# Mixture-of-experts tiles on one core: the down projection one tile later, and each transpose in front of a bf16 product

## The chip, the cores and the metric

The kernel runs on one core of a Trainium2 chip. A core has a matrix engine (TensorE, PE in the profile, with its weight loads as PEld), a vector engine (VectorE, DVE), a scalar engine (ScalarE, ACT), GpSimd (POOL), and SyncE (SP), which here only issues DMAs. Each engine works through its own list of instructions in order and waits on semaphores that the others raise. The metric is the device time of one execution in microseconds (us).

## The reference, cut to what matters

Eight sequences of 256 tokens of width 256 first pass a layer norm and a retention-like attention over a context. Then comes the part that this case is about, a layer of eight experts of which each token uses two:

```python
scores = softmax(xf @ Wg.T)                        # 2048 tokens, 8 experts
expert_weights, expert_indices = top_k(scores, 2)  # normalised to sum 1
h1 = xf @ W1[e].T + (xf @ A1[e].T) @ B1[e].T + b1[e]   # 256 -> 512
h3 = xf @ W3[e].T + (xf @ A3[e].T) @ B3[e].T + b3[e]   # 256 -> 512
g  = silu(h1) * h3
y_e = g @ W2[e].T + (g @ A2[e].T) @ B2[e].T + b2[e]    # 512 -> 256
y  = sum over the two experts of weight * y_e
x  = x + tanh(g_ffn) * y
```

## The kernel before

**The first stage** (to about 112 us) runs the attention for the eight sequences. Beside it the low-rank factors are folded into the expert weights: DVE adds a product of the factors to a staged weight unit, ACT rounds the sum to WH (`weight_hi`, L752), and POOL takes the rest as a bf16 part WL (`weight_lo`, L992). The six units of the last expert (number 7) are folded inside the first three expert tiles.

**The second stage** sorts the 4096 token-expert pairs by expert and works on 39 tiles (`NT_SLOTS`) of 128 rows, tile i with one expert. For one tile:

- POOL gathers 128 normalised rows of xn2 from memory into one of four buffers `xg` by an indirect DMA (`gather`, L1034 and L1056).
- PE transposes them, two f32 transposes of 128x128 into bank 0 (L630). ACT copies the result as a rounded `xh` (L877) and as bf16 `xb` (L878), and DVE takes the rest `xl` (L1493). There are two sets of these.
- PE forms h1 in bank 1 and h3 in bank 2 (`up`, L640). Each is six products of 512 columns: two with xh, two with xl, both against WH, and two with bf16 xb against WL.
- DVE adds the biases (L1503), ACT applies silu (L945), DVE multiplies into `g` (L1509).
- PE transposes g, four f32 transposes into bank 3 (L648). ACT makes `gh` (L883) and bf16 `gb` (L887), DVE the rest `gl` (L1497). There is one set of these.
- PE forms y in bank 4 (`down`, L657): twelve products of 256 columns, four each with gh, gl and gb.
- ACT has put the scaled output bias in `ys` (`scaled_bias`, L929), DVE adds y times the gate (`result`, L1515), and POOL adds the 128 rows to the output in memory with an indirect DMA (`scatter`, L1067 for its column of row numbers, L1079 for the DMA).

**What orders the work.** Everything is written out by hand; each engine has a function `tile(i, ...)` that is called for i = 0 to 38. On PE a step is: h1 of tile i, the transposes of g of tile i-1, the transposes of x of tile i+1, h3 of tile i, down of tile i-1. On POOL a step is the gather for tile i+3, in the first three steps a pair of `weight_lo` of the last expert, and the scatter of tile i-1. Two rules tie the scatters to the rest. A scatter waits until the scatter before it has landed (`pool.wait_ge(s_scat[1 - p], ...)`), since both add to rows in memory. And `ys` has two buffers, so that `scaled_bias` of a tile waits until the scatter of two tiles before has landed:

```python
if i >= 2:
    act.wait_ge(s_scat[p], 16 * half(i, p))
nc.scalar.activation(ys[p][:], b2, ACT.Copy, scale=gs[q]).then_inc(s_b2g, 1)
```

SP loads one row set of biases per tile for the first 16 tiles (`load_biases`, a broadcast to 128 partitions), and then the biases of all eight experts one after the other; from tile 5 on each such load also waits for the scatter of five tiles before. In step 4 ACT loads two tables of functions, once for exp and once back for silu.

Of the kernel before, what the change touches and what calls it, by code (L numbers as in the profile page):

```python
# [34 lines left out]
P = 128  # L35
B, S, D = 8, 256, 256
E, HID, R, K = 8, 512, 16, 2
TOK = B * S
NJ = TOK // P
CH = D // P  # L40
HC = HID // P
TPB = S // P
NT_SLOTS = TOK * K // P + E - 1
XBUF = 4
# [36 lines left out]
def flamingo(nc, x, ctxT, wqkv, tables, mask, gates_in, w_all, lora, biases, wgT, ident_in, consts, out):  # L81
# [9 lines left out]
    with whole:  # L91
# [255 lines left out]
        def _(sp):  # L347
# [63 lines left out]
            def load_biases(i):  # L411
# [21 lines left out]
                else:  # L433
                    sp.wait_ge(s_h3b, i - BRING + 1)
                    sp.wait_ge(s_b2g, i - BRING + 1)
                if i == 4:
                    sp.wait_ge(s_scat[0], 16)
                if i > BRING:
# [32 lines left out]
        def _(pe):  # L471
# [150 lines left out]

            def x_transposes(i, q):
                pe.wait_ge(s_xg[q], 16 * ((i - q) // XBUF + 1))
                if i > 0:
                    pe.wait_ge(s_xh, i)
                    pe.wait_ge(s_xb, i)
                    pe.wait_ge(s_xl, i)
                for c in range(CH):
                    last = nc.tensor.transpose(pX[:, c * P:(c + 1) * P], xg[q][:, c * P:(c + 1) * P], ident[:])  # L630
                last.then_inc(s_xT, 1)

            def up(dst, i, p, e, kind, sig):

                pos_wait(pe, s_h1b if kind == 0 else s_h3b, i)
                for part, (lhs, W, ready) in enumerate(((xh, WH, s_xh), (xl, WH, s_xl), (xb, WL, s_xb))):
                    if kind == 0:
                        pe.wait_ge(ready, i + 1)
                    for c in range(CH):
                        last = nc.tensor.matmul(dst[:, :], lhs[p][:, c * P:(c + 1) * P],  # L640
                                                W[:, bass.ds(e * (UNITS * UC) + (2 * kind + c) * UC, HID)],
                                                start=(part == 0 and c == 0), stop=(part == 2 and c == CH - 1))
                last.then_inc(sig, 1)

            def g_transposes(i):
                pe.wait_ge(s_g, i + 1)
                for c in range(HC):
                    last = nc.tensor.transpose(pG[:, c * P:(c + 1) * P], g[:, c * P:(c + 1) * P], ident[:])  # L648
                last.then_inc(s_gT, 1)

            def down(i, e):

                pos_wait(pe, s_ys, i)
                for part, (lhs, W, ready) in enumerate(((gh, WH, s_gh), (gl, WH, s_gl), (gb, WL, s_gb))):
                    pe.wait_ge(ready, i + 1)
                    for c in range(HC):
                        last = nc.tensor.matmul(pY[:, 0:D], lhs[:, c * P:(c + 1) * P],  # L657
                                                W[:, bass.ds(e * (UNITS * UC) + 4 * UC + c * D, D)],
                                                start=(part == 0 and c == 0), stop=(part == 2 and c == HC - 1))
                last.then_inc(s_y, 1)  # L660
# [12 lines left out]
            def tile(i, q, first, more):  # L673
                p = q % 2
                up(pH1, i, p, expert(q), 0, s_h1)
                if not first:
                    g_transposes(i - 1)
                if more:
                    x_transposes(i + 1, (q + 1) % XBUF)
                if first:  # L680
                    pe.wait_ge(s_wl, (E - 2) * UNITS + 4)
                up(pH3, i, p, expert(q), 1, s_h3)
                if more:
                    read_expert(i + 1, (q + 1) % XBUF)
                if not first:
                    if i == 1:
                        pe.wait_ge(s_wl, (E - 1) * UNITS)
                    down(i - 1, expert((q - 1) % XBUF))
                if i == 0:
# [23 lines left out]
            read_expert(0, 0)  # L713
            x_transposes(0, 0)
            keep_clock(4, WL, pS)
            pe.wait_ge(s_wl, (E - 2) * UNITS + 2)
            pe.wait_ge(s_top, 2 * (B - 1))
            tile_steps(pe, tile)
            g_transposes(NT_SLOTS - 1)
            down(NT_SLOTS - 1, expert((NT_SLOTS - 1) % XBUF))  # L720


        @block.scalar
        def _(act):
# [206 lines left out]
            def tile(i, q, first, more):  # L931
                p = q % 2
                v, at = places
                if not first:
                    g_high(i - 1)
                if more:
                    x_parts(i + 1, 1 - p)
                first_gate(i, q, v)
                if not first:
                    g_short(i - 1)  # L940
                if i == 2:
                    act.wait_ge(s_xn2Tp, B)
                    copy_xn2T(pO)
                act.wait_ge(s_h1b, i + 1)
                nc.scalar.activation(h1[:], h1[:], ACT.Silu).then_inc(s_silu, 1)  # L945
                both_gates(i, q, v)
                if not first:
# [41 lines left out]
        def _(pool):  # L989
# [102 lines left out]
            for i in range(NT_SLOTS):  # L1092
                if i + XBUF - 1 < NT_SLOTS:
                    gather(i + XBUF - 1)
                if i < 3:
                    weight_lo(E - 1, 1, 2 * i)
                    weight_lo(E - 1, 1, 2 * i + 1)
                if i >= 1:
                    scatter(i - 1)
            scatter(NT_SLOTS - 1)  # L1100
# [3 lines left out]
        def _(dve):  # L1104
# [412 lines left out]
            def tile(i, q, first, more):  # L1517
# [8 lines left out]
                biased(h1, pH1, i, x, 0, s_h1, s_h1b)  # L1526
                if not first:
                    g_rest(i - 1)
                if more:
                    x_rest(i + 1, 1 - p)  # L1530
                beside_h3(i)
                product(i, x)
                if not first:
                    result(i - 1, (q - 1) % XBUF)

            dve.wait_ge(s_x2, B)
            variance(st2, mv2, s_mv2, sums(x2, st2))
            x_rest(0, 0)
            tile_steps(dve, tile)
            g_rest(NT_SLOTS - 1)  # L1540
            result(NT_SLOTS - 1, (NT_SLOTS - 1) % XBUF)
# [71 lines left out]
```

## Time and profile before

| what | value |
|---|---|
| device time, median of three runs | 330.6 us (329.95 to 330.95) |
| span of the profiled execution, first to last instruction | 325.4 us |
| PE busy | 297.9 us, 92% of the span |
| DVE busy | 248.2 us, 76% |
| ACT busy | 206.0 us, 63% |
| POOL busy | 210.8 us, 65% |
| scatters | 39, each 1.66 us on POOL; POOL stood idle before them for 58.4 us in all |

The device time holds some 5.2 us that lie outside the span. Busy times are shares of the whole span and mix the two stages. A line of the profile gives engine, line of the kernel, operation and what is written from what. Ends of matmuls are modelled, so that the distance between two starts is the safer reading; where a row groups several matmuls, its start is that of the first.

### The profile page before, as it was taken

The page shows a single profiled execution, that of the slowest core. Times are in us where ns is not written, and L with a number is a line of the kernel's source. Part 1 is how long each engine was busy: PE and PEld are TensorE (multiplying, and loading weights), DVE is VectorE, ACT ScalarE, POOL GpSimd, SP SyncE. Part 2 cuts the span into 40 slices and gives each one's busy share as a digit, 9 for nine tenths or more (in the row PEclk, how much of TensorE's full clock was granted, in tenths as well). Part 3 has the DMA queues.
Part 4 walks back from the last instruction along what each step waited for, and adds up shares of the span by engine and source line. Part 5 has one row for each costly group of instructions (what it writes and reads, how often), then busy time and mean ns, then how long its engine had stood idle before and what let it go on. Part 6 is the DMA issues. An engine that isn't in the chain of part 4 may idle for free. (4 is left out here: it accounts for less than half of the span.)

```text
span 325.4 us, 7435 instructions
## 1 busy us (share of the span) xinstructions
PE 297.9 (92%) x1755; PEld 230.0 (71%) x1755; DVE 248.2 (76%) x607; ACT 206.0 (63%) x486; POOL 210.8 (65%) x246
## 2 busy tenths in 40 slices
PE   7589989999997798999999999999999999999960
PEld 3468778788886656776777777777777777777740
DVE  2679879889999998697988976767776776777750
ACT  5635755766878577787675565665675665675550
POOL 2457878888893098866756656766577776666241
PEclk9799999999999699999999999999999999999996
DMA  7968997999972169567747675766533223333100
GB/s 265 391 158 240 280 297 253 294 279 278 278 244 85 17 225 296 138 201 200 205 139 206 175 187 186 175 187 197 148 56 55 52 51 66 53 45 61 20 0 0
DMA packets 30424, 54.35 MB, mean 167 GB/s; under 512 B 7232, under 2 KB 15808, under 8 KB 30112
## 3 DMA queue, kind: packets, MB, share of 16 engines
q1 hardware_dynamic: 14672, 36.10, 34.1%
q0 software_dynamic: 7488, 9.36, 16.7%
q10 hardware_dynamic: 8224, 8.42, 8.6%
q8 instruction: 17, 0.28, 0.4%
q14 instruction: 23, 0.19, 0.2%
HBM read 41.92 MB, written 10.65 MB: 162 GB/s over the span
## 5 line engine op out<-in xcount | busy, mean ns | idle before, releaser
L1079 POOL DMA_INDIRECT out<-ys,cols x39 | 64.7, 1660 | 58.4 <-DMA out<-ys,cols 33.0
L883 ACT ACTIVATE gh<-bank 128x512 fp32r<-128x512 f32 x39 | 23.4, 599 | 61.0 <-PE bank L648 61.0
L640 PE MATMUL bank<-WH,xh 128*128 x156 | 55.7, 438 | 0.1
L1056 POOL DMA_INDIRECT xg<-xn_rows,colg x39 | 40.0, 1026 | 20.5 <-POOL colg L1034 10.3
L992 POOL TENSOR_TENSOR WL<-stage,WH 128x512 bf16<-128x512 f32 x38 | 47.9, 1278 | 7.3 <-ACT WH L752 7.1
L640 PE MATMUL bank<-WH,xl 128*128 x156 | 49.0, 395 | 0.0
L640 PE MATMUL bank<-WL,xb 128*128 x156 | 47.2, 385 | 0.0
L752 ACT ACTIVATE WH<-stage 128x512 fp32r<-128x512 f32 x38 | 22.9, 628 | 17.7 <-DVE stage L1110 14.5
L640 PEld LDWEIGHTS bank<-WH,xl 128*128 128x128 f32 x156 | 29.2, 188 | 6.8 <-DVE xl L1493 0.4
L1497 DVE TENSOR_TENSOR gl<-bank,gh 128x512 fp32r<-128x512 f32 x39 | 26.9, 689 | 8.8 <-ACT gh L883 8.7
L657 PE MATMUL bank<-WH,gh 128*128 x156 | 32.0, 327 | 1.5 <-ACT gh L883 1.5
L1509 DVE TENSOR_TENSOR g<-g,h 128x512 f32<-128x512 f32 x39 | 27.1, 694 | 5.0 <-ACT h L945 1.1
L1503 DVE TENSOR_TENSOR h<-bank,BA 128x512 f32<-128x512 f32 x23 | 15.9, 691 | 19.3 <-PE bank L640 18.1
L657 PEld LDWEIGHTS bank<-WH,gh 128*128 128x128 f32 x156 | 24.0, 190 | 7.7 <-issue 2.7
L1110 DVE TENSOR_TENSOR stage<-bank,stage 128x512 f32<-128x512 f32 x38 | 24.6, 676 | 0.9 <-DMA stage<-w_all_in 0.9
L657 PE MATMUL bank<-WH,gl 128*128 x156 | 24.9, 281 | 0.4 <-DVE gl L1497 0.4
L640 PEld LDWEIGHTS bank<-WH,xh 128*128 128x128 f32 x156 | 24.0, 190 | 1.7 <-issue 0.7
L648 PEld LDWEIGHTS bank<-ident,g 128*128 128x128 f32 x156 | 19.3, 140 | 8.1 <-DVE g L1509 1.1
L887 ACT ACTIVATE gb<-gh 128x512 bf16<-128x512 f32 x39 | 24.9, 638 | 0.0
L945 ACT ACTIVATE h<-h 128x512 f32<-128x512 f32 x39 | 24.9, 638 | 0.0
L640 PEld LDWEIGHTS bank<-WL,xb 128*128 128x128 bf16 x156 | 9.0, 98 | 21.3 <-issue 21.3
L657 PE MATMUL bank<-WL,gb 128*128 x156 | 23.8, 275 | 0.0
(229 smaller groups left out, 702.2 us busy)
## 6 DMA issues: line engine op xcount, KB each, us to landing
BB<-biases_in SPq DMA_DIRECT2D x16, 640.0 KB, 4.1
stage<-w_all_in SPq DMA_DIRECT2D x38, 256.0 KB, 5.1
BA<-biases_in SPq DMA_DIRECT2D x8, 640.0 KB, 3.9
WL<-w_all_in SPq DMA_DIRECT2D x10, 256.0 KB, 4.7
LS<-WH SPq DMA_DIRECT2D x45, 48.0 KB
xn_rows<-xn ACTq DMA_DIRECT2D x8, 256.0 KB, 4.1
out<-x ACTq DMA_DIRECT2D x7, 256.0 KB, 3.1
cx<-ctxT_in ACTq DMA_DIRECT2D x6, 256.0 KB, 6.5
```

Source lines behind the costliest of these rows:

```text
L640: last = nc.tensor.matmul(dst[:, :], lhs[p][:, c * P:(c + 1) * P], W[:, bass.ds(e * (UNITS * UC) + (2 * kind + c) * UC, HID)], start=(part ...
L657: last = nc.tensor.matmul(pY[:, 0:D], lhs[:, c * P:(c + 1) * P], W[:, bass.ds(e * (UNITS * UC) + 4 * UC + c * D, D)], start=(part == 0 and ...
L752: nc.scalar.activation(w_dst(WH, s, m), stage[stage_of(s * UNITS + m)][:, :], ACT.Copy).then_inc(s_wh, 1)
L883: nc.scalar.activation(gh[:], pG[:, :], ACT.Copy).then_inc(s_gh, 1)
L887: nc.scalar.activation(gb[:], gh[:].bitcast(F32), ACT.Copy).then_inc(s_gb, 1)
L945: nc.scalar.activation(h1[:], h1[:], ACT.Silu).then_inc(s_silu, 1)
L992: nc.gpsimd.tensor_tensor(w_dst(WL, s, m), stage[stage_of(s * UNITS + m)][:, :], w_dst(WH, s, m).bitcast(F32), ALU.subtract).then_inc(s_wl, 1)
L1056: nc.gpsimd.indirect_dma_start(out=xg[q][:], out_offset=None, in_=xn2_d[0:JA * P, :] if i < NA else xn2_d, in_offset=bass.IndirectOffsetOn ...
L1079: nc.gpsimd.indirect_dma_start(out=out_rows, out_offset=bass.IndirectOffsetOnAxis(ap=cols[:, i:i + 1], axis=0), in_=ys[p][:], in_offset=No ...
L1110: nc.vector.tensor_tensor(stage[b][:, :], pW[m % 2][:, :], stage[b][:, :], ALU.add).then_inc(s_add, 1)
L1497: nc.vector.tensor_tensor(gl[:], pG[:, :], gh[:].bitcast(F32), ALU.subtract).then_inc(s_gl, 1)
L1509: nc.vector.tensor_tensor(g[:], g[:], h1[:], ALU.mult).then_inc(s_g, 1)
```

## The change

On PE the down projection of a tile moves one step later and to another place: step i holds h1 of tile i, down of tile i-2, h3 of tile i. The two transposes of x of tile i+1 are no longer a block; each stands in front of one of the two bf16 products of h1. The four transposes of g of tile i-1 stand in front of the four bf16 products of the down projection of tile i-2. After the last step down of tile 37, the transposes of g of tile 38 and its down remain.

On ACT the making of gh and gb of tile i-1 moves from the start of the step and from behind the first gate to a place behind the silu of tile i. On DVE the rest gl of tile i-1 moves behind the result, which is now that of tile i-2, and the product h3 times silu comes last. On POOL the scatter in step i is that of tile i-2. SP drops one wait: the bias load of tile 4 no longer waits for the scatter of tile 0.

```diff
@@ SP, load_biases
-                if i == 4:
-                    sp.wait_ge(s_scat[0], 16)
                 if i > BRING:
                     sp.wait_ge(s_scat[(i - BRING - 1) % 2], 16 * ((i - BRING - 1) // 2 + 1))
@@ PE
+            def x_transpose(i, c):
+                q = i % XBUF
+                if c == 0:
+                    pe.wait_ge(s_xg[q], 16 * ((i - q) // XBUF + 1))
...
+            def g_transpose(i, c):
+                if c == 0:
+                    pe.wait_ge(s_g, i + 1)
...
+            def up(dst, i, p, e, kind, sig, x_next=None):
...
                     for c in range(CH):
+                        if part == 2 and x_next is not None:
+                            x_transpose(x_next, c)
...
-            def down(i, e):
+            def down(i, e, g_next=None):
...
                     for c in range(HC):
+                        if part == 2 and g_next is not None:
+                            g_transpose(g_next, c)
...
             def tile(i, q, first, more):
                 p = q % 2
-                up(pH1, i, p, expert(q), 0, s_h1)
-                if not first:
-                    g_transposes(i - 1)
-                if more:
-                    x_transposes(i + 1, (q + 1) % XBUF)
+                up(pH1, i, p, expert(q), 0, s_h1, i + 1 if more else None)
+                if i == 1:
+                    for c in range(HC):
+                        g_transpose(0, c)
+                if i == 2:
+                    pe.wait_ge(s_wl, (E - 1) * UNITS)
+                if i >= 2:
+                    down(i - 2, expert((q - 2) % XBUF), i - 1)
...
                 up(pH3, i, p, expert(q), 1, s_h3)
...
-                    down(i - 1, expert((q - 1) % XBUF))
...
             tile_steps(pe, tile)
-            g_transposes(NT_SLOTS - 1)
+            down(NT_SLOTS - 2, expert((NT_SLOTS - 2) % XBUF))
+            for c in range(HC):
+                g_transpose(NT_SLOTS - 1, c)
             down(NT_SLOTS - 1, expert((NT_SLOTS - 1) % XBUF))
@@ ACT, tile
-                if not first:
-                    g_high(i - 1)
                 if more:
                     x_parts(i + 1, 1 - p)
                 first_gate(i, q, v)
-                if not first:
-                    g_short(i - 1)
...
                 nc.scalar.activation(h1[:], h1[:], ACT.Silu).then_inc(s_silu, 1)
+                if not first:
+                    g_high(i - 1)
+                    g_short(i - 1)
                 both_gates(i, q, v)
@@ POOL, the loop over tiles
-                if i >= 1:
-                    scatter(i - 1)
+                if i >= 2:
+                    scatter(i - 2)
+            scatter(NT_SLOTS - 2)
             scatter(NT_SLOTS - 1)
@@ DVE, tile
                 biased(h1, pH1, i, x, 0, s_h1, s_h1b)
-                if not first:
-                    g_rest(i - 1)
                 if more:
                     x_rest(i + 1, 1 - p)
                 beside_h3(i)
+                if i >= 2:
+                    result(i - 2, (q - 2) % XBUF)
+                if not first:
+                    g_rest(i - 1)
                 product(i, x)
-                if not first:
-                    result(i - 1, (q - 1) % XBUF)
```

On PE, a late step before, from h1 through the transposes to the start of h3 (bank 1 is h1, bank 2 h3, bank 3 the transposed g, bank 0 the transposed x; ISA sets an address register):

```order
L640 MATMUL bank1<-WH,xl1 128x512 x2
L640 ISA
L640 MATMUL bank1<-WL,xb1 128x512
L640 ISA
L640 MATMUL bank1<-WL,xb1 128x512
L648 MATMUL bank3<-ident,g 128x128 x4
L630 MATMUL bank0<-ident,xg2 128x128 x2
L640 ISA
L640 MATMUL bank2<-WH,xh1 128x512
```

The same place now, from the xl products of h1 to the first product of the down projection (bank 4):

```order
L649 MATMUL bank1<-WH,xl1 128x512 x2
L629 MATMUL bank0<-ident,xg2 128x128
L649 ISA
L649 MATMUL bank1<-WL,xb1 128x512
L629 MATMUL bank0<-ident,xg2 128x128
L649 ISA
L649 MATMUL bank1<-WL,xb1 128x512
L662 ISA
L662 MATMUL bank4<-WH,gh 128x256
```

The two transposes of x have moved from behind h1 into its last third, one in front of each bf16 product, and what follows h1 is now the down projection.

On POOL, the second and third step of the tile loop before, from the second pair of `weight_lo` to the second scatter (xg are gathered rows, colg and cols the row numbers of a gather and of a scatter):

```order
L992 TENSOR_TENSOR WL<-stage,WH 128x512 x2
L1030 TENSOR_LOAD vid
L1030 ISA x2
L1067 ISA
L1067 COPY cols<-sidxA 128x1
L1079 DMA out<-ys,cols 2048x256
L1030 TENSOR_LOAD vid
L1030 ISA x2
L1034 ISA
L1034 COPY colg<-gidxA 128x1
L1056 DMA xg<-xn_rows,colg 128x258
L992 TENSOR_TENSOR WL<-stage,WH 128x512 x2
```

The same place now, from the second pair of `weight_lo` to the first scatter:

```order
L998 TENSOR_TENSOR WL<-stage,WH 128x512 x2
L1036 TENSOR_LOAD vid
L1036 ISA x2
L1040 ISA
L1040 COPY colg<-gidxA 128x1
L1062 DMA xg<-xn_rows,colg 128x258
L998 TENSOR_TENSOR WL<-stage,WH 128x512 x2
L1036 TENSOR_LOAD vid
L1036 ISA x2
L1073 ISA
L1073 COPY cols<-sidxA 128x1
L1085 DMA out<-ys,cols 2048x256
```

The first scatter has moved behind the next gather and behind the third pair of `weight_lo`, to the place that the second scatter had before.

## Rows read from the trace of the kernel before

**Rows 1.** The page, its first line.
```profile
span 325.4 us, 7435 instructions
```

**Rows 2.** Chain of waits, one late step: start us, us, what.
```profile
236.50 0.44 PE bank L648 x4
...
237.16 1.38 PE bank L640 x6
238.54 1.39 PE bank L657 x12
...
241.31 0.44 PE bank L648 x4
```

**Rows 3.** Timeline of PE, before tile 0: start, duration, instruction, [idle <- releaser].
```profile
117.06 0.38 PE L630 MATMUL bank<-ident,xg 128*128 128x128 f32 x2
117.28 1.03 PE L475 MATMUL bank<-WL 128*128 128x512 bf16 x4
```

**Rows 4.** Timeline of PE, three stops in the tile stage.
```profile
125.34 0.44 PE L630 MATMUL bank<-ident,xg 128*128 128x128 f32 x2 [1.44 <-DMA xg<-xn_rows,colg]
...
149.06 0.78 PE L657 MATMUL bank<-WH,gh 128*128 x4 [0.62 <-ACT gh L883]
...
184.90 0.50 PE L657 MATMUL bank<-WH,gl 128*128 x2 [0.41 <-DVE gl L1497]
```

**Rows 5.** Timeline of POOL, the first three scatters and the last pair of weight_lo.
```profile
132.56 1.63 POOL L1079 DMA_INDIRECT out<-ys,cols  x1 [0.95 <-POOL cols L1067]
...
135.86 2.52 POOL L992 TENSOR_TENSOR WL<-stage,WH 128x512 bf16<-128x512 f32 x2
...
139.32 1.60 POOL L1079 DMA_INDIRECT out<-ys,cols  x1 [0.81 <-issue]
...
144.70 1.90 POOL L1079 DMA_INDIRECT out<-ys,cols  x1 [2.07 <-ACT gsel L901]
```

**Rows 6.** Line L1079, issue to landing: all 39 scatters.
```profile
DMA to landing us min/median/max: 2.7/4.1/5.8
```

**Rows 7.** Line L1079, issue to landing: the 16 scatters from 149.3 to 226 us.
```profile
DMA to landing us min/median/max: 3.7/4.7/5.8
```

**Rows 8.** Timeline of POOL, the fourth and the nineteenth scatter.
```profile
149.36 1.60 POOL L1079 DMA_INDIRECT out<-ys,cols  x1 [1.07 <-DMA out<-ys,cols]
...
225.45 1.74 POOL L1079 DMA_INDIRECT out<-ys,cols  x1 [1.16 <-DMA out<-ys,cols]
```

**Rows 9.** Timeline of ACT, end of step 2, then step 4 and start of step 5.
```profile
134.78 1.16 ACT L752 ACTIVATE WH<-stage 128x512 fp32r<-128x512 f32 x2
...
144.54 0.51 ACT L929 ACTIVATE ys<-BB,gsel 128x256 f32<-128x256 f32 x1
...
148.22 0.58 ACT L883 ACTIVATE gh<-bank 128x512 fp32r<-128x512 f32 x1
```

**Rows 10.** Timeline of PE: h3 of tile 6, then transposes of g of tiles 6 and 20.
```profile
152.93 0.71 PE L640 MATMUL bank<-WH,xh 128*128 x2
...
157.17 0.60 PE L648 MATMUL bank<-ident,g 128*128 128x128 f32 x4
...
226.69 0.49 PE L648 MATMUL bank<-ident,g 128*128 128x128 f32 x3
```

**Rows 11.** Groups by line, 207 to 300 us: busy us, mean ns, idle before.
```profile
L1509 DVE TENSOR_TENSOR g<-g,h 128x512 f32<-128x512 f32 x19 | 13.2, 692 | 2.3 <-ACT h L945 0.5
...
L1515 DVE SCALAR_TENSOR_TENSOR ys<-bank,gsel,ys 128x256 f32<-128x256 f32 x19 | 9.2, 484 | 3.1 <-ACT ys L929 2.9
L1493 DVE TENSOR_TENSOR xl<-bank,xh 128x256 fp32r<-128x256 f32 x19 | 8.0, 423 | 0.0
...
L877 ACT ACTIVATE xh<-bank 128x256 fp32r<-128x256 f32 x19 | 7.2, 378 | 0.0
```

**Rows 12.** PE by stretches: us, busy (instructions), granted clock, DMA share, GB/s.
```profile
8.90:12.30 3.40, 0.17 (x2) 1.00 1.04 384
12.30:15.70 3.40, 3.40 (x9) 0.50 1.05 402
```

**Rows 13.** Timeline of POOL, the last scatter but one.
```profile
313.66 1.57 POOL L1079 DMA_INDIRECT out<-ys,cols  x1 [2.79 <-DVE ys L1515]
```

More of the change, by code:

```diff
@@ L621, in _ @@
             pX, pH1, pH3, pG, pY = bank[0], bank[1], bank[2], bank[3], bank[4]
[L623 to L633, printed above, removed]
+            def x_transpose(i, c):
+                q = i % XBUF
+                if c == 0:
+                    pe.wait_ge(s_xg[q], 16 * ((i - q) // XBUF + 1))
+                    if i > 0:
+                        pe.wait_ge(s_xh, i)
+                        pe.wait_ge(s_xb, i)
+                        pe.wait_ge(s_xl, i)
+                turned = nc.tensor.transpose(pX[:, c * P:(c + 1) * P], xg[q][:, c * P:(c + 1) * P], ident[:])
+                if c == CH - 1:
+                    turned.then_inc(s_xT, 1)
+            def g_transpose(i, c):
+                if c == 0:
+                    pe.wait_ge(s_g, i + 1)
+                turned = nc.tensor.transpose(pG[:, c * P:(c + 1) * P], g[:, c * P:(c + 1) * P], ident[:])
+                if c == HC - 1:
+                    turned.then_inc(s_gT, 1)
+            def up(dst, i, p, e, kind, sig, x_next=None):
                 pos_wait(pe, s_h1b if kind == 0 else s_h3b, i)
@@ L643, in up @@
                 last.then_inc(sig, 1)
[L645 to L649, printed above, removed]
-            def down(i, e):
+            def down(i, e, g_next=None):
                 pos_wait(pe, s_ys, i)
@@ L684, in tile @@
                     read_expert(i + 1, (q + 1) % XBUF)
-                if not first:
-                    if i == 1:
-                        pe.wait_ge(s_wl, (E - 1) * UNITS)
-                    down(i - 1, expert((q - 1) % XBUF))
                 if i == 0:
@@ L713, in _ @@
             read_expert(0, 0)
-            x_transposes(0, 0)
+            for c in range(CH):
+                x_transpose(0, c)
             keep_clock(4, WL, pS)
@@ L1531, in tile @@
                 beside_h3(i)
+                if i >= 2:
+                    result(i - 2, (q - 2) % XBUF)
+                if not first:
+                    g_rest(i - 1)
                 product(i, x)
-                if not first:
-                    result(i - 1, (q - 1) % XBUF)
             dve.wait_ge(s_x2, B)
@@ L1539, in _ @@
             tile_steps(dve, tile)
+            result(NT_SLOTS - 2, (NT_SLOTS - 2) % XBUF)
             g_rest(NT_SLOTS - 1)
```

## The prediction, made blind

> **What bounds the kernel now.** I read the page first, then the chain of waits, the timeline of PE for its stops, the timeline of POOL and the landing times of the scatters, and last the timeline of ACT around the one long stop. The chain of waits of a late step [rows 2] shows PE alone: six transposes from 236.50 to 237.16 (0.66 us), six products of h3 (1.38), twelve products of down (1.39), six of h1 (the 1.38 up to 241.31). The step is 4.81 us and nothing in it waits. So PE bounds the late tiles, and only a shorter row of PE instructions makes them faster.
>
> Earlier tiles have a second limit beside it. A scatter may start only when the one before has landed. From the fourth scatter (149.36) to the nineteenth (225.45) nearly every one waits for exactly that [rows 8], fifteen intervals in 76.09 us, 5.07 us each; landing takes 4.7 us there [rows 7]. That chain is slower than a PE step. It stays hidden only as long as the work can run ahead of it, and `ys` has two buffers, so the lead is limited. PE's stops in the tile stage are few: 1.44 us for gathered rows, 0.62 for gh, 0.41 for gl [rows 4].
>
> **The change part by part.**
>
> *Transposes in front of bf16 products.* PE does the same 6 transposes and 24 products per tile. What could be gained is the time that a transpose or a weight load stands exposed. In a block, six transposes take 0.66 us, 0.11 each [rows 2]. The trace has one place where two transposes stand between bf16 products: 117.06 to 117.28, 0.22 for two, the second followed at once by a bf16 product [rows 3]. So a transpose costs 0.11 there too, and moving it frees nothing. What is left is small and of unknown sign: products of one size stand a little apart by what precedes them (twelve of down in 1.39 are 0.116 each, where a transpose takes 0.11 [rows 2]), so that six pairs may be worth 0.03 us per tile either way. I take a gain of 0.015, since the two bf16 groups now follow a transpose instead of a product of another kind.
>
> The Trainium skill (TensorE: Matmul & The Clock Gate, section LDWEIGHTS (loading the stationary operand)) gives a weight load as the number of columns over 1.2 GHz, 107 ns for 128, and in section Back-to-back issue gap about 56 ns for an isolated product of 128 columns; bf16 weights it counts among those that load faster (Weight-path perf modes). By that a block of transposes is held by its loads, each would cost 56 ns between products, and the step would fall by six times 0.05, some 0.3 us (an estimate from that page). The trace does not agree: with a bf16 product behind it instead of another f32 load, the transpose takes 0.11 all the same [rows 3]. What the mechanism would give is the second rival.
>
> *Down two tiles behind.* What it buys is slack. gh, gl and gb of a tile are now needed one h3 and one h1 later, so stops like the 0.62 and the 0.41 [rows 4] should go by themselves. Against that stands the first stop. The transposes of x of tile 2 wait for gathered rows until 125.34 [rows 4]. Before, all of h1 of tile 1 and the transposes of g of tile 0 ran ahead of that stop; now two bf16 products (0.44) and the transposes of g (0.44 [rows 2]) stand behind it: +0.9 us at the start, which is inside the total below.
>
> *The scatters on POOL.* This is the part that decides. The first scatter stood behind the second pair of `weight_lo` and issued at 132.56. Now it stands behind the third pair. That pair ran at 135.86, and the second scatter followed at 139.32 [rows 5]. The pair waits for ACT's last weight units, at 134.78 before [rows 9]; in the new order ACT comes to them at much the same time, since its step 2 hangs on h1 of tile 2 as before. So the first scatter now issues at about 139.0 instead of 132.56: the whole chain of scatters starts one scatter late, about 6.5 us, while the result of a tile comes only some 3.4 us later than before (h1, six transposes and down, 1.38 + 0.66 + 1.39 [rows 2]).
>
> What waits for it: the scaled bias of tile 3 needs the scatter of tile 1 landed. Before, that scatter issued at 139.32 and ACT wrote ys at 144.54 without a stall worth the name [rows 5, 9]. Now: 139.0 plus 4.1 to land [rows 6], 0.4 until the next issue (5.07 less 4.7 [rows 7, 8]; it is the second scatter that counts), plus 4.7, 148.2. Behind that wait on ACT stand the two table loads of step 4: from the ys to the next large instruction it took 148.22 - 144.54 = 3.68 us [rows 9]. And behind these now stands xh of tile 6, which before stood behind gh. So xh starts at 151.9 and is ready at 152.3 (0.38 [rows 11]). PE would want it for h1 of tile 6 at about 149.8 (h3 of tile 6 was at 152.93 [rows 10]; 0.9 later for the start, 0.6 earlier without the stop at 149.06, and 3.43 back over h1, transposes and down), so it stops for 2.5 us. From 152.3 on: DVE has xl after xb at 153.0 (0.42 [rows 11]), h1 ends at 154.2. DVE still has ys (0.48), then gl once gh is there at 153.9, and the two steps of g (0.69 each [rows 11]), to 156.1; PE wants g at 155.1, a second stop of 1.0. Four transposes of g with four bf16 products take 0.9, and h3 of tile 6 starts at 157.0. At that point both kernels have done the same work (down up to tile 4, h1 up to 6); before, it was 152.93 [rows 10]. So +4.1 us; with both landings as short as 3.7 it is +2.7, with one of 5.8 it is +5.2.
>
> *Tiles 6 to 20.* The kernel before takes 157.17 to 226.69 for fourteen steps, 4.97 each, stops and some routing products included [rows 10]. If the chain of scatters holds each step to 5.07, that is +1.4; if it never binds again, the 0.41 stop goes and the transposes give their 0.03 fourteen times, -0.8. I take 0: PE has just lost 4 us to the chain, so it starts with little lead, but the lead that it has then is what the chain needs.
>
> *Tiles 20 to 38, and the end.* The scatters no longer bind there; 18 steps at 0.015 give -0.3. At the end, the scatter of tile 36 now issues when h3 of tile 38 ends instead of one down earlier, and the scatter of tile 37 (before at 313.66, waiting for its own ys [rows 13]) has to wait for its landing; between 0 and +1.2, I take +0.3.
>
> *SP.* The dropped wait lets one bias load go early, which would otherwise sit behind the later first scatter: 0. The bias load of tile 5 still waits for that first scatter, lands about 147.5 and is needed at 146; the DVE idle time between h1 and the result covers it, and if not, it falls into the stop that ACT makes anyway.
>
> Sum: 4.1 + 0 - 0.3 + 0.3 = +4.1. The profiled execution has a span of 325.4 us [rows 1], and with the 5.2 outside it that is the median, 330.6; I forecast 334.7.
>
> **Rivals.**
>
> *1. ACT's slack swallows the late scatter (no change).* For it: x is now transposed early in h1, so xh has nearly three us of lead, and every later use of gh and gl has more than two. If two landings and the gap come to less than 6.6 us, so that the scatter of tile 1 has landed by 145.6, ys is no later than its own place and PE does not stop. That needs 3.1 each; the shortest of all is 2.7, but only at the very end where nothing else moves, and in the bias loads' stretch the least is 3.7 [rows 6, 7]. Then: stops -1.0 [rows 4], transposes -0.6, start +0.9, end +0.3: 330.2.
>
> *2. The transposes are hidden (faster).* Six products of 512 columns take 1.38, 0.23 each [rows 2], so 128 columns by themselves would take a quarter, 0.06; if the other 0.05 of a transpose is a weight load that a long product in front of it can cover, a step falls by 0.3 us wherever PE bounds. If the chain of scatters still costs its 4.1, the gain counts only in the last 18 steps, -5.4: 329.3. Without that cost it would be 38 steps, some -11: 319. It decides from a transpose at 0.09 instead of 0.11 on. Rows 3 speak against it, with a single instance.
>
> *3. The clock falls in the long stop.* Early in the program a stretch with PE busy for 0.17 of 3.4 us was followed by one at a granted clock of 0.50, that is 1.2 GHz, for 3.4 us [rows 12]. Two stops of 3.5 us in all in step 6 come near to it; at half the clock for 3.4 us or twice that, PE falls back by 1.7 to 3.4: 336.4 to 338.1. Against it: before the stop and between the two PE is at work with full products.
>
> *4. The chain keeps binding.* Gathers on POOL stand behind scatters, bias loads wait for scatters of five tiles before; with the chain late by one scatter these become stops of their own in tiles 6 to 20, +1.4 to +4: 336 to 338.6.
>
> **How the numbers follow.** The forecast (332 to 336) has a chance of 0.55, rival 1 (329.6 to 331.6) 0.14, rival 2 (below 329.6) 0.13, rival 3 0.09, rival 4 0.09. Of rival 1 a part falls on either side of 0.3% (1.0 us), which is about what a measurement of this kernel can tell from no change. So faster by over 0.3%: 0.15, within: 0.13, slower: 0.72. The likeliest case alone ranges from 332.0 to 336.0; the range for 8 in 10 goes down to 329.6, into rivals 1 and 2, and up to 338.0, through most of 3 and 4.
>
> **What would show it.** Right: the first scatter issues near 139 instead of 132.6; ACT waits for a scatter before the ys of tile 3 until about 148; PE stands idle for more than 2 us before h1 of tile 6, released by ACT's xh; the transposes of g of tile 6 come some 4 us late in absolute time; late steps of 4.78 to 4.81 us, the transposes still 0.11 behind the product that follows. Wrong: late steps of 4.5 to 4.7 us (rival 2); no stop of PE over 1 us behind step 2, with ACT's wait before that ys under 1 us (rival 1); a granted clock of 0.50 in the tile stage (rival 3). I would be wrong altogether if the third pair of `weight_lo` ran well before 135, since then the chain of scatters would start early enough.

## The result, and the profile after

The changed kernel takes 333.7 us (median of 18 runs, 331.1 to 337.9), the kernel before 330.5 on the same chip (18 runs, 328.0 to 333.1): a ratio of 1.009, with an interval of 1.006 to 1.012, so 2.1 to 3.9 us slower. The forecast was 334.7. Executions of any kernel here that come out over 1.5% above its fastest are left out of the ratios; where few remain, the interval is wide. Single profiles scatter by microseconds, so profiles show below which wait is where, and ratios what it costs.

The page, first line, answering [rows 1]:

```profile
span 331.5 us, 7472 instructions
```

The spans differ by 6.1 us, twice what the times do. 1.7 of it lies ahead of the change (the first transposes of x start at 118.76, before at 117.06 [rows 3]). And in all runs that list both numbers, 1.75 to 3.0 us of the time lie outside the span, not the 5.2 that were taken: the profile of before probably caught a short execution.

Timeline of POOL in the changed kernel, from the third pair of `weight_lo` to the third scatter (start, duration, instruction, [idle before <- what ended it]), answering [rows 5]:

```profile
135.87 2.92 POOL L998 TENSOR_TENSOR WL<-stage,WH 128x512 bf16<-128x512 f32 x2 [1.12 <-ACT WH L759]
...
139.87 1.62 POOL L1085 DMA_INDIRECT out<-ys,cols  x1 [0.95 <-DVE ys L1522]
...
144.04 1.60 POOL L1085 DMA_INDIRECT out<-ys,cols  x1 [0.81 <-DMA out<-ys,cols]
...
148.94 2.06 POOL L1085 DMA_INDIRECT out<-ys,cols  x1 [1.61 <-DMA out<-ys,cols]
```

The first scatter issues at 139.87, where 139.0 was said and 132.56 stood before. Timeline of ACT, steps 3 and 4, answering [rows 9]:

```profile
143.85 0.51 ACT L936 ACTIVATE ys<-BB,gsel 128x256 f32<-128x256 f32 x1 [3.54 <-DMA out<-ys,cols]
...
148.78 0.51 ACT L936 ACTIVATE ys<-BB,gsel 128x256 f32<-128x256 f32 x1 [0.44 <-DMA out<-ys,cols]
149.30 1.28 ACT L971 ACT_TABLE_LOAD   x1
...
151.06 1.28 ACT L974 ACT_TABLE_LOAD   x1
...
152.46 0.37 ACT L884 ACTIVATE xh<-bank 128x256 fp32r<-128x256 f32 x1
```

ACT stands 3.54 us in front of the ys of tile 2, until the first scatter has landed (139.87 and 3.9 to land, 143.8), and 0.44 in front of that of tile 3. The two table loads follow, and only behind them xh of tile 6. Over the whole program ACT's ys now waits nearly five times as long as before (3.8 us in 6 waits there). Waits of the changed kernel: engine, line, what for, us in all, times, longest:

```profile
ACT ys L936 <- DMA out<-ys,cols: 17.7, 16, 3.5
...
PE bank L636 <- DVE g L1516: 4.2, 8, 0.9
```

Timeline of PE, its stops up to tile 6, answering [rows 4], and the start of h3 of tile 6, answering [rows 10]:

```profile
126.04 0.30 PE L629 MATMUL bank<-ident,xg 128*128 128x128 f32 x1 [1.48 <-issue]
...
145.73 0.22 PE L591 MATMUL bank<-HB,trimB 128*128 128x128 bf16 x1 [0.89 <-DVE HSB L1371]
...
146.38 0.73 PE L649 MATMUL bank<-WH,xh 128*128 x2 [0.38 <-DVE h L1510]
...
149.66 0.30 PE L636 MATMUL bank<-ident,g 128*128 128x128 f32 x1 [0.48 <-DVE g L1516]
...
153.08 0.73 PE L649 MATMUL bank<-WH,xh 128*128 x2 [0.98 <-ACT xh L884]
...
156.56 0.30 PE L636 MATMUL bank<-ident,g 128*128 128x128 f32 x1 [0.56 <-DVE g L1516]
...
157.38 0.71 PE L649 MATMUL bank<-WH,xh 128*128 x2
```

What was forecast as one stop of 2.5 us and one of 1.0 comes as five of 0.4 to 1.0. In the first two PE waits for DVE, which is late with routing work: it has waited for values (idxf) that ACT writes behind the late ys of tile 2. Timeline of DVE:

```profile
144.59 0.24 DVE L1367 TENSOR_TENSOR OHB<-cst,idxf 128x64 bf16<-128x64 f32 x1 [2.66 <-ACT idxf L772]
```

h3 of tile 6 starts at 157.38 (157.0 was said); less the 1.7 of the first stage that is 2.75 us later than before.

The chain of waits, one late step (start us, us, what), answering [rows 2]:

```profile
263.12 2.30 PE bank L649 x10
265.42 0.11 PE bank L629
265.53 0.22 PE bank L649
...
266.07 0.95 PE bank L662 x8
267.02 0.11 PE bank L636
267.13 0.11 PE bank L662
...
267.90 2.31 PE bank L649 x10
```

The step is 4.78 us (267.90 less 263.12), before 4.81 [rows 2]. Single steps differ by some hundredths: over the ten from h3 of tile 26 to h3 of tile 36 a step is 4.78 us here and 4.84 before. A transpose takes 0.11 in front of a product as it did in a block. The granted clock is 1.00 from 119 to 310 us.

### The profile page after: what moved, and what is told of

It is laid out like the page before. It is cut to its first block and busy times, and to the rows that moved or that the text cites. A ratio compares the mean times of both kernels' runs of the same rounds, so it can differ in the third digit from the quotient of the medians.

```text
span 331.5 us, 7472 instructions
## 1 busy us (share of the span) xinstructions
PE 298.5 (90%) x1755; PEld 237.0 (71%) x1755; DVE 248.7 (75%) x607; ACT 215.3 (65%) x486; POOL 208.8 (63%) x246
## 5 line engine op out<-in xcount | busy, mean ns | idle before, releaser
L649 PE MATMUL bank<-WH,xh 128*128 x156 | 58.8, 457 | 1.4 <-ACT xh L884 1.0
L649 PE MATMUL bank<-WL,xb 128*128 x156 | 50.9, 382 | 0.0
L636 PE MATMUL bank<-ident,g 128*128 128x128 f32 x156 | 35.8, 274 | 4.3 <-DVE g L1516 4.2
L662 PE MATMUL bank<-WL,gb 128*128 x156 | 35.5, 273 | 0.0
L649 PEld LDWEIGHTS bank<-WH,xh 128*128 128x128 f32 x156 | 26.2, 190 | 7.6 <-issue 2.7
L884 ACT ACTIVATE xh<-bank 128x256 fp32r<-128x256 f32 x39 | 14.9, 382 | 20.2 <-PE bank L629 11.9
L636 PEld LDWEIGHTS bank<-ident,g 128*128 128x128 f32 x156 | 21.6, 140 | 7.3 <-issue 5.5
L1522 DVE SCALAR_TENSOR_TENSOR ys<-bank,gsel,ys 128x256 f32<-128x256 f32 x39 | 18.7, 479 | 10.6 <-PE bank L662 10.5
L1500 DVE TENSOR_TENSOR xl<-bank,xh 128x256 fp32r<-128x256 f32 x39 | 16.3, 417 | 12.9 <-ACT xb L885 12.7
```

What stands on the lines that cost most here:

```text
L636: turned = nc.tensor.transpose(pG[:, c * P:(c + 1) * P], g[:, c * P:(c + 1) * P], ident[:])
```

## The experiments

The late scatter alone, the early first scatter, the late scaled bias and the blocks ran on one chip (kernel before: 332.9 us); x of tile 2 back, the row places, the changed kernel once more and the free bias loads on another (332.1); the three turns on a third (331.3); the last kernel on a fourth (331.6). So times are compared as ratios to the kernel before on the same chip. "Expected" was written before each run.

**The late scatter alone, in the kernel before.** Only POOL's place of the scatter and SP's wait are changed.

```diff
-                if i >= 1:
-                    scatter(i - 1)
+                if i >= 2:
+                    scatter(i - 2)
+            scatter(NT_SLOTS - 2)
```

> The kernel before, with only POOL's part of the change: in step i it scatters tile i-2, and the bias load of tile 4 does not wait for the first scatter. PE, ACT and DVE keep the old order. Theory: the first scatter issues near 139, ACT waits some 4 us before the ys of tile 2, and since gh stands behind that ys in the old order and has less slack, the time rises to 334 to 337. Rivals 1 and 2: POOL's place for the scatter is hidden, 330 to 331.5.

Measured 336.5 us, 1.0146 times before (1.007 to 1.022), as expected. Timeline of ACT, ys of tile 2:

```profile
145.87 0.51 ACT L927 ACTIVATE ys<-BB,gsel 128x256 f32<-128x256 f32 x1 [3.32 <-DMA out<-ys,cols]
```

The same wait in the same place, without any new order on PE, and a cost no smaller than that of the whole change. The place of the scatters is a sufficient cause.

**The first scatter back in front of the third pair of `weight_lo`,** in the changed kernel.

```diff
+                if i == 2:
+                    scatter(0)
...
-                if i >= 2:
+                if i >= 3:
                     scatter(i - 2)
```

> The changed kernel, but in the third step of the tile loop POOL issues the first scatter ahead of the third pair of weight_lo instead of behind it. Theory (the chain of scatters starts one scatter late, ACT then waits for landings before it may write ys, and PE waits for ACT): the first scatter issues near 134 instead of 139.9, ACT's waits for scatters before ys fall from 17.7 us to under 5, PE's stops in tiles 4 to 6 go, and the time falls from 333.7 to 327.5 to 330, below the kernel before. Rival 1 (the cost lies in the new order on PE and DVE, where the product of g comes behind the result and the rest gl): stays at 333 to 334.5. Rival 2 (the transposes between bf16 products cost PE time): stays at 333 to 334.5.

Measured 333.1 us, 1.003 times before (0.998 to 1.008): some two thirds of the loss are gone (though this interval and that of the changed kernel, 1.006 to 1.012, overlap), but the time is not below that of before, which the theory had expected. The first scatter issues at 136.20, 3.7 us earlier than in the changed kernel (3.0 counted from the first transposes of x). Waits of this kernel, and PE by one stretch (us, busy, granted clock, DMA share, GB/s):

```profile
ACT ys L936 <- DMA out<-ys,cols: 6.7, 8, 1.8
```

```profile
127.20:130.60 3.40, 3.40 (x12) 0.52 0.74 280
```

The stretch begins 1.2 us behind a stop of 2.06 us at x of tile 2. For 3.4 us PE has half its clock (1.2 GHz), which costs 1.7 us of its work; no wait for a scatter stands in front of that stop.

**And the transposes of x of tile 2 back behind those of g of tile 0,** on top of the last.

```diff
-                up(pH1, i, p, expert(q), 0, s_h1, i + 1 if more else None)
+                up(pH1, i, p, expert(q), 0, s_h1, i + 1 if more and i != 1 else None)
...
                         g_transpose(0, c)
+                    for c in range(CH):
+                        x_transpose(2, c)
```

> The changed kernel with two things put back: the scatter of tile 0 stands ahead of POOL's third pair of weight_lo, and in step 1 the transposes of x of tile 2 stand as a block behind the transposes of g of tile 0, as before, so that the wait for gathered rows comes 0.9 us of work later. Theory A (the start term is a real 0.9 us of its own): the stop before the transposes of x of tile 2 falls from about 2.0 us to about 1.2, and the time is 0.5 to 1.2 us below what the early scatter alone gave, 0.998 to 1.002 of the kernel before. Rival B (the stop is absorbed, since the tiles from 4 on go by the chain of scatters and by DVE): the stop becomes shorter but the stops on g and xh in steps 4 to 6 grow by as much, and the time is that of the early scatter alone, 1.002 to 1.005 of the kernel before.

Measured 333.8 us, 1.005 times before (1.002 to 1.009), as rival B had it. The stop at x of tile 2 shrinks from 2.06 to 1.50 us, and another grows. Timeline of POOL: the first scatter, the third pair, the second scatter:

```profile
137.19 1.99 POOL L1087 DMA_INDIRECT out<-ys,cols  x1 [0.96 <-POOL cols L1075]
138.64 3.10 POOL L1000 TENSOR_TENSOR WL<-stage,WH 128x512 bf16<-128x512 f32 x2
...
144.47 1.61 POOL L1087 DMA_INDIRECT out<-ys,cols  x1 [0.81 <-issue]
```

Timeline of ACT, ys of tile 3; timeline of PE, h1 of tile 6:

```profile
148.50 0.51 ACT L938 ACTIVATE ys<-BB,gsel 128x256 f32<-128x256 f32 x1 [1.80 <-DMA out<-ys,cols]
```

```profile
152.80 0.73 PE L649 MATMUL bank<-WH,xh 128*128 x2 [2.01 <-ACT xh L886]
```

The pair of `weight_lo` now stands in front of the second scatter, ys of tile 3 waits for it, the table loads and xh of tile 6 stand behind, and PE stops for 2.01 us: from the ys of tile 3 on this is the path that was forecast, one tile later than in the changed kernel. Behind the stop PE again has half the clock for 3.4 us (154.2 to 157.6, granted 0.51).

**And ACT's reading of row places moved** from the end of the step to behind the first gate, on top of the last.

```diff
                 first_gate(i, q, v)
+                if more:
+                    read_places(i + 1)
...
-                if more:
-                    read_places(i + 1)
```

> As the kernel with both things put back, and ACT's reading of the next tile's row places moved from the end of the step to behind the first gate, so that it no longer stands between a ys that was late and the xh that PE waits for. Theory A: the register loads cost ACT 0.6 to 0.9 us in front of xh, so PE's stop on xh of tile 6 goes and the time falls by 0.3 to 1.0 us. Rival B (DVE, and not ACT, holds tiles 5 to 12, by g): the stop on xh is smaller, the stops on g are larger, the time stays within 0.3 us of the kernel without this edit.

Measured 332.6 us, 1.0036 times before (1.000 to 1.007). The stop on xh of tile 6 is 1.94 us, against 2.01: theory A named the wrong thing in front of xh. It is the wait for the landing and the table loads. The difference in time, 1.3 us, is inside both intervals. Behind this stop, too, PE has half the clock:

```profile
152.80:156.20 3.40, 3.40 (x13) 0.51 0.74 203
```

So each of the three profiles with an early first scatter has such a stretch ahead of h3 of tile 6. Less its 1.7 us, the way to there takes 36.1, 36.7 and 36.2 us, where the kernel before took 35.9: in these profiles the half clock is most of what is left of the loss there.

**The scaled bias one step later,** so that ACT need not wait (from step 4 on, behind silu).

```diff
                 nc.scalar.activation(h1[:], h1[:], ACT.Silu).then_inc(s_silu, 1)
+                if i >= 4:
+                    scaled_bias(i - 2, (q - 2) % XBUF, held[0])
...
-                if not first:
+                if i in (1, 2):
                     scaled_bias(i - 1, (q - 1) % XBUF, at)
```

> The changed kernel, but from step 4 on ACT writes the scaled bias of tile i-2 behind the silu of tile i instead of that of tile i-1 at the end of the step, some 3 us later and just ahead of the result that needs it. The chain of scatters starts as late as in the changed kernel. Theory: a landing has 3 us more, ACT's waits before ys fall from 17.7 us to 4 to 8, and the time to 329.5 to 332. Rival 1: unchanged, 333 to 334.5. Rival 2: unchanged, 333 to 334.5.

Measured 336.3 us, 1.015 times before (1.007 to 1.023): the expectation was wrong. Waits of this kernel:

```profile
DVE ys L1527 <- ACT ys L937: 28.1, 34, 1.2
...
PE bank L636 <- DVE g L1521: 5.4, 9, 1.0
```

ACT's wait is gone, and DVE's result now waits in nearly every tile for an ys that ACT writes only just ahead of it; behind the result stand the rest of g and the next g, for which PE stops. Tiles 6 to 20 are the slowest but one of the table below. Up to h3 of tile 6, though, this kernel takes 36.4 us against 38.6 of the changed one, with the first scatter as late as there (141.13, 21.9 us behind the first transposes of x; 21.1 there). So the loss up to that point does run through ACT's wait in front of ys.

**The transposes in blocks** again, in the changed kernel: x behind h1, g in front of the gb products.

```diff
-                        if part == 2 and x_next is not None:
-                            x_transpose(x_next, c)
...
+                if x_next is not None:
+                    for c in range(CH):
+                        x_transpose(x_next, c)
```

> The changed kernel, but the transposes stand in blocks again: the two of x behind all six products of h1, the four of g ahead of the four bf16 products of down. Theory: a transpose costs 0.11 us in either place, the late step goes from 4.78 back to 4.81 to 4.82, the time to 334 to 335.5. Rival 2 (transposes between bf16 products cost time): late step below 4.75, time 332 or less. If transposes were hidden between products after all: late step above 4.95 and the time over 337.

Measured 338.0 us, 1.012 times before (1.000 to 1.025; four runs, which decide nothing on the time). The chain of waits, one late step:

```profile
266.21 0.44 PE bank L636 x4
266.64 0.44 PE bank L664 x4
267.08 2.76 PE bank L647 x12
269.84 0.22 PE bank L629 x2
270.06 0.94 PE bank L664 x8
271.00 0.44 PE bank L636 x4
```

4.79 us, where the interleaved step has 4.78. Four transposes in a block take 0.44, and four single ones 0.11 each: nothing is hidden. Over the ten steps from h3 of tile 26 on a step is 4.793 us here, 4.779 in the changed kernel and 4.836 before. So 0.014 goes with the place of the transposes, and the other 0.043 with the rest of the new order, which on PE is the late down projection.

**The changed kernel once more,** on the second chip.

> The changed kernel itself once more, as the yardstick for the three other runs on this chip. My theory: 1.006 to 1.012 times the kernel before, with ACT waiting some 3.5 us in front of ys of tile 2 and the waits of ACT's ys for scatters at 15 to 19 us in all.

Measured 336.9 us, 1.0125 times before (1.006 to 1.019); ACT waits 3.47 us at the ys of tile 2, and 13.3 in front of all ys (15 to 19 was expected). This execution has something that the first did not. Timeline of PE, x of tile 2; then PE by stretches (us, busy, granted clock, DMA share, GB/s):

```profile
125.54 0.45 PE L629 MATMUL bank<-ident,xg 128*128 128x128 f32 x1 [2.77 <-issue]
```

```profile
122.00:125.40 3.40, 0.77 (x4) 0.98 1.05 329
125.40:128.80 3.40, 3.26 (x11) 0.52 0.80 267
```

The stop at the gathered rows is 2.77 us, and behind it 3.4 us run at half the clock, 1.2 GHz: 1.7 us of work lost. That was rival 3, at another stop than the one named.

**Bias loads that don't wait for scatters,** in the changed kernel.

```diff
-                if i > BRING:
-                    sp.wait_ge(s_scat[(i - BRING - 1) % 2], 16 * ((i - BRING - 1) // 2 + 1))
```

> The changed kernel, in which the bias loads of tiles 5 to 15 no longer wait for the scatter of five tiles before; nothing else is changed. Theory A (the chain of scatters reaches PE only through ACT's ys): the time stays within 0.3% of the changed kernel, and ACT's waits in front of ys stay at 15 to 19 us. Rival B (the prediction's fourth rival: bias loads held back by the late scatters are stops of their own): the time falls by 1.4 us or more.

Measured 343.4 us, 1.0375 times before (1.033 to 1.043): neither theory. With the wait, SP's load goes out when a scatter has landed, in one instance 0.05 us ahead of the next scatter (190.80 and 190.85). Without it, timelines of SP and POOL:

```profile
193.41 0.34 SPq L436 DMA_DIRECT2D BB<-biases_in  x1
```

```profile
192.85 1.60 POOL L1083 DMA_INDIRECT out<-ys,cols  x1 [2.27 <-DMA out<-ys,cols]
```

The load comes 0.56 us behind the scatter's issue. Issue to landing of the scatters from 160 to 200 us, of the changed kernel and of this one:

```profile
DMA to landing us min/median/max: 4.2/4.6/5.4
```

```profile
DMA to landing us min/median/max: 5.3/5.5/7.4
```

In the median a scatter lands 0.9 us later, and since the next one waits for it, the whole chain is slower: tiles 6 to 20 take 77.7 us instead of 71.3. PE is busy for 70.6 of these 77.7 us and waits for DVE's g and ACT's xh, not for gathered rows: a slow chain does hold PE. In the changed kernel it is busy for 68.9 of 71.3 us, so there the chain can cost it 2.4 us at most.

**Turning to the new order in mid-way,** at step 6, 12 or 22; the step of the turn has no down projection.

```diff
+                late = i >= TURN_AT
...
+                if i > TURN_AT:
                     down(i - 2, expert((q - 2) % XBUF), i - 1)
...
+                if not first and not late:
+                    down(i - 1, expert((q - 1) % XBUF))
```

> The kernel before up to step 5 and the changed order from step 6 on: step 6 has no down projection, result or scatter, since all of tile 4 is done by then; the bias load of tile 4 waits as before. Theory A (the loss is made by the first scatters alone): the first scatter stands near 132.6 us as before, ACT's ys shows no wait over 1 us in tiles 2 to 5, the start term, the stop on xh of tile 6 and the 3 us are gone, and the gain of the late steps is left, 0.05 to 0.07 us in each of the 18 steps in which PE alone binds: 0.8 to 1.3 us below the kernel before, 0.996 to 0.998 of it. Rival B (the changed order costs in the tiles held by the chain of scatters as well, since g, its rest and ys stand later in DVE's and ACT's rows): stops on g of 0.5 us and more between steps 7 and 20 eat the gain, and the time is 1.000 to 1.006.

> As the last one, with the changed order from step 12 on. Theory A: as with step 6, 0.996 to 0.998 of the kernel before. Rival B: half of what it costs in tiles 6 to 20 is left, 0.998 to 1.003.

> As the last one, with the changed order from step 22 on, behind the last scatter that waits for the one before. Both theories: the late steps gain 0.05 to 0.07 us each and the end loses 0.1, so 0.7 to 1.0 us below the kernel before, 0.997 to 0.998 of it; the late step in the trace is 4.78 us against 4.84. If the gain of the late steps were only a matter of that one profile, the step would be 4.84 and the time that of the kernel before.

Measured 1.0002 (0.997 to 1.003), 0.996 (0.989 to 1.003; two of nine runs) and 1.004 (1.001 to 1.007) times before. With the turn at step 6 the loss is gone, which fits theory A, but the gain is not there: rival B's figure. With the turn at step 22 the time is above what either theory gave (0.997 to 0.998), though its late steps have the 4.78 us: its profile has a PE stop of 2.34 us at the turn and 3.4 us at half the clock behind it. The turn itself costs. With the turn at step 6, timeline of PE, x of tile 8, and timeline of POOL, the gather of its rows:

```profile
158.43 0.30 PE L632 MATMUL bank<-ident,xg 128*128 128x128 f32 x1 [1.49 <-issue]
```

```profile
152.44 0.77 POOL L1054 CAST colg<-gidxA 128x1 uint32 x1
153.48 1.00 POOL L1076 DMA_INDIRECT xg<-xn_rows,colg  x1 [0.27 <-POOL colg L1054]
```

PE arrives a down projection early, and the gather stands behind a scatter that waited 1.93 us for a landing. So the last run moved that step's transposes of x behind the down projection:

```diff
+                if i == TURN_AT + 1:
+                    for c in range(CH):
+                        x_transpose(i + 1, c)
```

> The kernel that turns to the changed order at step 6, with one edit: in step 7 the two transposes of x of tile 8 stand as a block behind the down projection of tile 5, 1.8 us later, instead of inside h1. Theory A (the stop of 1.5 us at x of tile 8 came from the switch itself: step 6 has no down projection, PE reaches the next transposes of x 1.4 us early, and their gather stands on POOL behind a scatter that waits): that stop goes, nothing takes its place, and the time is 0.8 to 2 us below the kernel that turned at step 6 without this, 0.994 to 0.998 of the kernel before. Rival B (the chain of scatters holds tiles 6 to 20 at its own pace, whatever PE does in between): the stop is turned into stops on g or on x of the next tiles, and the time stays 0.998 to 1.002.

That stop goes, one of 0.36 us is left a tile later, and the time is 333.4 us, against 331.6 before (six runs from 327.5 to 336.7, too far apart for a verdict). None of these versions is shown to be faster than the kernel before.

The profiles side by side, in us, between the start of the first transposes of x, the start of h3 of tile 6, that of h3 of tile 20 and the last landing (differences of starts in that kernel's timeline; the last scatter lands 2.7 us behind its start). In rows with a star 3.4 us of the first column ran at half the clock:

| kernel | to h3 of tile 6 | tiles 6 to 20 | to the end |
|---|---|---|---|
| before | 35.9 | 69.5 | 97.4 |
| changed | 38.6 | 71.3 | 97.3 |
| changed, once more * | 41.6 | 70.0 | 96.6 |
| early first scatter * | 37.8 | 70.1 | 96.6 |
| early, x of tile 2 back * | 38.4 | 68.8 | 96.6 |
| early, x back, places moved * | 37.9 | 69.7 | 97.4 |
| late scatter in before | 39.5 | 72.9 | 97.5 |
| late scaled bias | 36.4 | 74.7 | 97.3 |
| free bias loads * | 41.9 | 77.7 | 98.3 |
| turn at step 22: order of before up to tile 21 | 35.9 | 73.0 | 100.7 |

## Why the prediction was right, and where not

The time, its sign and the cause were right. The term of 4.1 us (scatters on POOL) is the only one of size, and experiments on both sides carry it. The late scatter alone costs as much in the kernel before; an earlier first scatter brings 1.009 down to 1.003 to 1.005; with the old order up to step 5 the loss is gone (1.0002).

Its path was one tile off. The prediction put the long wait at the ys of tile 3, for the second scatter. The wait came at the ys of tile 2, for the first scatter; the step missed that the ys of tile 2 asks for buffer 0, whose scatter had moved by the same 7 us. Behind this ys stand no table loads but routing values, so that the loss comes in five small stops. With the first scatter and x of tile 2 put back, a wait of 1.80 us stands at the ys of tile 3, where the prediction had it; with the first scatter alone put back there is none at that ys.

Its size: 4.1 was taken for the way to h3 of tile 6, and 2.75 and 5.8 are measured in two executions. Of the 3.0 between these, 1.3 is the stop at x of tile 2 (1.48 and 2.77 by the rows) and 1.7 the half clock behind the longer one. The start term of 0.9 is in the direction said (1.44 before [rows 4]) but varies more than it weighs.

Tiles 6 to 20 were taken as 0, as a balance of two unknowns. +1.8 and +0.5 are measured, but that can't be put down to the change: the kernel that turns at step 22 runs these tiles in the order of before and takes 73.0 us, 3.5 more than the profile of before, with stops on gathered rows. What the rows show is that landings of 4.6 us in the median are as short as before [rows 7], and that DVE's g, now last in its row, makes PE stop for up to 0.9.

Late steps: 0.015 us each was said, for the transposes in front of bf16 products, and that is what goes with them (0.014 by the run with blocks). The late down projection, which the forecast put at nothing, gives another 0.043; over ten steps that is 4.84 before and 4.78 after. The end, from h3 of tile 20 on, is 0.1 and 0.8 us shorter, for 0.0 said.

The terms as the two profiles have them add up to 4.4 and 5.4 us over the profile of before, and the ratio of the times gives 2.1 to 3.9. That the sum of 4.1 came so near is in part luck, since a profile is one execution and the one of before was probably short.

Rival 1 (slack swallows it) fell by the wait of 3.54 us. Rival 2 (hidden transposes) fell by the transposes of 0.11 us in front of a product, and by the run with blocks. By the estimate that the prediction draws from the Trainium skill (TensorE: Matmul & The Clock Gate, section LDWEIGHTS (loading the stationary operand)) the transposes would have saved 0.3 us per step; the trace does not agree, the run with blocks shows 0.014. Rival 3 (the clock) is not in the first profile and is in the second, at x of tile 2; at the stop that it named, in front of h1 of tile 6, it came in three of the other kernels. So its chance of 0.09 looks too low. Rival 4 (bias loads and gathers as stops of their own) fell: freeing the bias loads costs 6.5 us (343.4 against 336.9 on that chip), and PE does not wait for gathered rows in tiles 6 to 20 of the changed kernel.

Open: why the tiles 6 to 20 differ by 1.3 us between two executions of the changed kernel and by 3.5 between two of the old order, and whether an order with this late step and the early scatters of before can be reached without the stop at the turn. Three buffers of ys should take ACT's wait away; that wasn't tried.

## What to carry to other kernels

Where transfers form a chain in which each waits for the last, the start of its first link is a due time: before an edit puts a step later, look at what it stands behind on the engine that issues the transfer, since one pair of slow instructions in front of the first link moved all of them. A wait taken off one engine turns up on the next one that needs the same buffer, as the late scaled bias showed. A gain of 0.06 us in each of the 18 steps where one engine binds (1.0 us) is worth no more than one stop of 1 us that the same edit makes at the start.

## What the runs showed of the hardware

**A transfer's neighbours by half a microsecond.** In the changed kernel seven of the eight scatters from 160 to 200 us have a load of 640 KB that goes out 0.05 to 0.7 us ahead of them, and the median to landing is 4.6 us. With free bias loads all seven there have it 0.56 us or more behind them, and the median is 5.5. Two scatters of the changed kernel have a load 0.3 and 0.5 us behind them (issued at 175.40 and 200.47) and take 5.0 and 6.8 us to land. Held back by a wait, the loads leave the program 6.5 us shorter.

**The clock after stops.** In the tile stage, 3.4 us at a granted clock of 0.50 to 0.52 (1.2 GHz) came behind PE stops of 2.77 (changed kernel, second execution), 2.34 (turn at step 22), 2.06 (early scatter), 2.01 (x of tile 2 back), 1.94 (places moved) and 1.86 us (free bias loads). None came behind stops of 2.91 (free bias loads), 2.22 (blocks), 2.21 (late scaled bias) and 1.98 us (turn at step 6, x moved), all four at x of tile 2. So a stop of about 2 us may cost 1.7 us more, and its length alone does not decide it.
